# Projections, overflow check and attention of a transformer block joined in one program block, and two more row groups normalised inside the attention

## What is computed

```
x = x + 0.5 * FFN(layernorm(x))      # "first FFN"
x = x + Attention(layernorm(x))
x = x + 0.5 * FFN(layernorm(x))      # "second FFN"
```

## Time and profile before

| | us |
|---|---|
| median of 3 runs | 1558.76 |
| the profiled execution's own time | 1560.47 |
| its span, first to last instruction | 1558.4 |
| first FFN, about | 0 to 490 |
| projections and overflow check | 490 to 583 |
| attention | 583 to 1095 |
| second FFN | 1095 to 1558 |

### The profile page before, as it was taken

How to read it: one execution, slowest core, us unless ns; L and a number is a source line. 1 busy time by engine, 2 the same in 40 slices (tenths; PEclk the granted TensorE clock), 3 DMA queues, 4 the chain that set the end, 5 groups by cost and what they waited for, 6 DMA issues and landing times. The chain is left out here.

```text
span 1558.4 us, 26615 instructions
## 1 busy us (share of the span) xinstructions
PE 1492.9 (96%) x9977; PEld 1043.3 (67%) x9977; DVE 895.8 (57%) x1963; ACT 976.9 (63%) x1332; POOL 549.6 (35%) x477
## 2 busy tenths in 40 slices
PE   4999999999997979999999999999899999999997
PEld 3788888888986863333343343343688889888896
DVE  6788776666755971231145152033788867666663
ACT  7322254455434869999999999998622245445542
POOL 2000255666544971211111111120300045666645
PEclk9999999999998998999999999999899999999999
DMA  8222266676646689415246063121511246666653
GB/s 279 76 67 68 84 175 153 148 153 158 147 80 157 230 273 182 85 19 84 35 90 136 30 125 59 25 69 41 167 50 62 69 153 150 151 151 150 162 113 41
DMA packets 121377, 181.05 MB, mean 116 GB/s; under 512 B 19040, under 2 KB 83040, under 8 KB 118496
## 3 DMA queue, kind: packets, MB, share of 16 engines
q1 hardware_dynamic: 92784, 130.56, 32.0%
q0 software_dynamic: 28464, 48.78, 15.3%
HBM read 123.73 MB, written 55.57 MB: 115 GB/s over the span
## 5 line engine op out<-in xcount | busy, mean ns | idle before, releaser
L2140 ACT ACTIVATE 8258_pr<-8258_pS 128x1024 f32<-128x1024 f32 x448 | 420.6, 1195 | 7.4 <-PE 8258_pS L2059 7.4
L2090 PE MATMUL 8258_pO<-8258_pr,6357_vres 128*32 128x512 f32 x1792 | 238.2, 605 | 0.0
L2059 PEld LDWEIGHTS 8258_pS<-sq_rows,sk_rows 50*128 50x128 f32 x896 | 77.9, 185 | 184.4 <-ACT 8258_pr L2140 133.4
L2059 PE MATMUL 8258_pS<-sq_rows,sk_rows 50*128 50x512 f32 x896 | 184.7, 470 | 6.6 <-PEq L1716 5.6
L346 PE MATMUL 115_pGU<-columns_XT,weights_wts 128*128 128x512 f32 x384 | 152.7, 398 | 1.0 <-DVE columns_XT L1118 0.8
L346 PE MATMUL 15280_pGU<-columns_XT,weights_wts 128*128 128x512 f32 x384 | 152.7, 398 | 1.0 <-DVE columns_XT L1118 0.8
L2153 POOL TENSOR_SCALAR_AFFINE_SELECT 8258_pr<-8258_pr 128x512 f32<-128x512 f32 x32 | 20.5, 641 | 371.1 <-ACT 8258_pr L2140 371.1
L347 PE MATMUL 15280_pGU<-columns_XT,weights_wts 128*128 128x512 f32 x384 | 149.7, 390 | 0.0
L347 PE MATMUL 115_pGU<-columns_XT,weights_wts 128*128 128x512 f32 x384 | 149.7, 390 | 0.0
L348 PE MATMUL 115_pGU<-columns_XT,weights_wts 128*128 128x512 f32 x384 | 149.6, 390 | 0.0
L348 PE MATMUL 15280_pGU<-columns_XT,weights_wts 128*128 128x512 f32 x384 | 149.6, 390 | 0.0
(11 more groups left out here) (393 smaller groups left out, 3491.3 us busy)
## 6 DMA issues: line engine op xcount, KB each, us to landing
115_raw_g<-WgT SPq DMA_DIRECT2D x16, 512.0 KB
115_raw_u<-WuT SPq DMA_DIRECT2D x16, 512.0 KB
115_raw_d<-WdT SPq DMA_DIRECT2D x16, 512.0 KB
q_rows<-rows_halves SPq DMA_DIRECT2D x8, 1024.0 KB, 4.9
k_rows<-rows_halves SPq DMA_DIRECT2D x8, 1024.0 KB, 5.1
15280_raw_g<-WgT SPq DMA_DIRECT2D x16, 512.0 KB
15280_raw_u<-WuT SPq DMA_DIRECT2D x16, 512.0 KB
15280_raw_d<-WdT SPq DMA_DIRECT2D x16, 512.0 KB
```

The costliest lines, as they stand in the source:

```text
L2059: m = t_.matmul(to[:, e, :], key, query, start=True, stop=True)
L2090: m = t_.matmul(pO[e * 32:(e + 1) * 32, j % 2, off:off + wd], vres[:, (g // GB) * TPB + kt, at:at + 32], from_(e), start=n == first[j], st ...
L2140: s_exp.done(a.activation(to, pS[:, u % RING, :, :], ACT.Exp, scale=HD ** -0.5))
```

## The change

- The three functions return their engine functions instead of opening a block, and `attn` puts them behind each other in one block. Where the barriers stood, an engine waits for the semaphores that it needs: all four checking engines for the flag, TensorE for the last rotations, squares and v copies, ScalarE for the last rotations and, at unit 7 (pair 4), for all lower parts, VectorE for the last v product ahead of its memset. Buffers move so that the first units write over nothing that is still read.
- The end of the projections is put in another order: unit 12's lower part goes from GpSimd to VectorE (`POOL_LOW` 12), the last two squares and rotations are interleaved, the norms stand between the halves of the last v product, and VectorE finds the flag before the lower parts of units 13 to 15. ScalarE loads the Exp table before its last v copy. TensorE issues 24 matmuls of ones (`FILL`).
- SyncE issues the second halves of heads 0 to 3 behind the stores of units 12, 13 (two) and 14.
- `READY` is 7: quads 5 and 6 are normalised in the attention, quad 6 into a buffer of its own (`apart`), without a wait for its store, and with two table stores. The second FFN normalises quad 7 alone, GpSimd splits one shared weight before its one table store and two behind it.

```diff
-AHEAD, READY = 4, 5
+AHEAD, READY, APART = 4, 7, 6
...
-            ring = lambda q: (q - (ready > 0)) % KN
+            ring = lambda q: (q - ready + AHEAD if ready else q) % KN
...
+
+            def row(q, j, cols):
+                if q == APART and q < ready:
+                    return self.apart[:, j // 2, :].rearrange("p (t d) -> p t d", d=D)[:, j % 2, cols]
+                return xn(q)[:, j, cols]
...
-                    deviation(ready)
-                    columns(0)
-                    deviation(ready + 1)
-                    normalize(ready)
-                    columns(1)
-                    normalize(ready + 1)
-                    deviation(ready + 2)
-                    columns(2)
-                    normalize(ready + 2)
-                    for q in range(3, J):
+                    for q in range(ready, J):
+                        deviation(q)
+                        if q > ready:
+                            normalize(q - 1)
+                        columns(q - ready)
...
-                    statistics(ready)
-                    statistics(ready + 1)
-                    scale(ready)
-                    low_columns(0)
-                    scale(ready + 1)
-                    statistics(ready + 2)
-                    low_columns(1)
-                    scale(ready + 2)
-                    for q in range(2, J):
+                    for q in range(ready, J):
+                        statistics(q)
+                        scale(q)
+                        low_columns(q - ready)
+                    for q in range(J - ready, J):
                         low_columns(q)
...
-                        s_wh.done(g.tensor_copy(weight(1, w, 0), raw[w][:, :, :]))
-                    s_wh.wait(g, w + 1)
+                        s_whs.done(g.tensor_copy(weight(1, w, 0), raw[w][:, :, :]))
+                        s_whs.wait(g, w + 1)
+                    else:
...
+                if ready:
+                    split_shared(0)
                 for q in range(ready, J):
-                    if ready:
-                        split_shared(q - ready)
                     g.wait_ge(*s_xn.at(q - ready + 1))
...
                 if ready:
-                    g.wait_ge(*self.s_table.at(READY))
+                    split_shared(1)
+                    split_shared(2)
+                    g.wait_ge(*self.s_table.at(READY + 1))
...
-            POOL_LOW = 2 * J - 3
+            POOL_LOW = 2 * J - 4
+            FILL = 24
+            REST_AFTER = ((6, 0), (6, 1), (6, 1), (7, 0))
...
+                        for hh, at in enumerate(REST_AFTER):
+                            if at == (q, half_):
+                                self.load_head(sp, 0, hh, slice(S // 2, S), self.s_rest)
...
                     s_sq.wait(t_, n - 2)
+                    s_turn.wait(t_, n - 2)
...
-                    values(q)
+                    if q + 1 < J:
+                        values(q)
+                values(J - 1, (0,))
                 norms(J - 1)
+                values(J - 1, (1,))
                 t_.wait_ge(*s_top.at(1))
                 s_tt.done(t_.transpose(pN[0:1, 0:P], top[:, :], self.ident[:, :]))
...
+                for _ in range(FILL):
+                    t_.matmul(pX[:, 0, 0:P], self.ones[:, :], self.ones[:, :], start=True, stop=True)
...
                 def square(n):
-                    a.wait_ge(*s_turn.at(n + 1))
...
-                    square(4 * q + 2)
-                    high(2 * q)
-                    square(4 * q + 3)
-                    value(q)
+                    if q + 1 < J:
+                        square(4 * q + 2)
+                        high(2 * q)
+                        square(4 * q + 3)
+                        value(q)
+                square(4 * J - 1)
+                square(4 * J - 2)
+                high(2 * J - 2)
+                value(J - 1, (0,))
+                a.activation(warm[:, :], self.eps[0:1, :], ACT.Exp)
+                value(J - 1, (1,))
                 high(2 * J - 1)
-                a.activation(warm[:, :], self.eps[0:1, :], ACT.Exp)
...
-                    v.wait_ge(*s_Q.at(n + 1))
+                    v.wait_ge(*(s_sq.at(n) if n == 4 * J - 1 else s_Q.at(n + 1)))
...
-                    s_lo.wait(v, n // 2 - 2)
+                    s_lo.wait(v, min(n // 2 - 2, POOL_LOW))
...
-                    rotate(4 * q + 2)
-                    rotate(4 * q + 3)
+                    if q + 1 < J:
+                        rotate(4 * q + 2)
+                        rotate(4 * q + 3)
...
                 k = (2 * J - 1) % 3
+                low(POOL_LOW)
+                v.wait_ge(*s_last.at(1))
+                rotate(4 * J - 2)
+                rotate(4 * J - 1)
                 s_turn.wait(v, 4 * J)
-                v.tensor_tensor(turns[k][:, 0, :], turns[k][:, 0, :], turns[k][:, 2, :], ALU.subtract)
-                s_last_y.done(v.tensor_tensor(turns[k][:, 1, :], turns[k][:, 1, :], turns[k][:, 3, :], ALU.add))
-                low(POOL_LOW)
                 largest(J - 1)
                 s_norm.wait(v, J // 2)
                 s_top.done(v.tensor_reduce(top[:, :], norm[:, :], AX.X, ALU.max))
-                low(POOL_LOW + 1)
+                v.tensor_tensor(turns[k][:, 0, :], turns[k][:, 0, :], turns[k][:, 2, :], ALU.subtract)
+                s_last_y.done(v.tensor_tensor(turns[k][:, 1, :], turns[k][:, 1, :], turns[k][:, 3, :], ALU.add))
                 v.wait_ge(*s_tt.at(1))
                 s_flag.done(v.tensor_reduce(best[:, :], pN[0:1, 0:P].rearrange("p (a h) -> p a h", a=2), AX.X, ALU.max))
                 v.wait_ge(*s_flag.at(1))
                 s_flag.done(v.tensor_tensor(prod[:, :], best[:, 0:1], best[:, 1:2], ALU.mult))
                 v.wait_ge(*s_flag.at(2))
                 s_flag.done(v.tensor_scalar(self.unsafe[:, :], prod[:, :], SAFE_NORMS, None, ALU.is_gt))
-                low(POOL_LOW + 2)
-                v.wait_ge(*s_flag.at(3))
-
...
+                for n in range(POOL_LOW + 1, 2 * J):
+                    low(n)
...
             def guarded(eng, body):
+                eng.wait_ge(*self.s_flag.at(3))
                 r = eng.value_load(self.unsafe[0:1, 0:1], min_val=0, max_val=1)
...
 
-            @blk.sync
-            def _(sp):
+            def on_sync(sp):
...
+                    sp.wait_ge(*self.s_kept.at(2 * NQ))
+                    sp.wait_ge(*self.s_last.at(2 * NQ - self.POOL_LOW))
...
+            self.apart = yb[:, :, APART % QB, :, :].rearrange("p c k d -> p c (k d)")
...
+                if m == APART:
+                    norm_at[quiet(max(root_at) + 4, 1)] = m
+                    table_at[max(norm_at) + 1] = m
+                    continue
...
-                for hh in range(GH):
-                    self.load_head(sp, 0, hh, slice(S // 2, S), self.s_rest)
...
                     sp.wait_ge(*self.s_norm.at(m + 1))
-                    self.s_table.done(sp.dma_start(table[m], mine_of(m)))
+                    if m == APART:
+                        for c in range(DC):
+                            self.s_table.done(sp.dma_start(table[m][:, 2 * c:2 * c + 2, :], self.apart[:, c, :].rearrange("p (t d) -> p t d", d=D)))
+                    else:
...
+                t_.wait_ge(*self.s_turned.at(4 * NQ))
+                t_.wait_ge(*self.s_squared.at(4 * NQ))
+                t_.wait_ge(*self.s_kept.at(2 * NQ))
...
+                a.wait_ge(*self.s_turned.at(4 * NQ))
                 for u, (kind, a_, b_) in enumerate(units):
                     a.wait_ge(*s_S.at(u + 1))
+                    if (kind, a_) == ("pair", 4):
+                        a.wait_ge(*self.s_low.at(self.POOL_LOW))
+                        a.wait_ge(*self.s_last.at(2 * NQ - self.POOL_LOW))
...
-                        to = prs[:, a_ % 2, 2 * b_:2 * b_ + 2, :]
+                        to = prs[:, (a_ + 1) % 2, 2 * b_:2 * b_ + 2, :]
...
                 def normalize(m):
-                    s_out[m % 4].wait(v, m // 4 + 1)
+                    if m != APART:
+                        s_out[m % 4].wait(v, m // 4 + 1)
                     for j in range(4):
-                        i = v.tensor_scalar(mine_of(m)[:, j, :], mine_of(m)[:, j, :], root[:, j:j + 1], shift[:, j:j + 1], ALU.mult, ALU.add)
+                        i = v.tensor_scalar(rows_of(m, j), mine_of(m)[:, j, :], root[:, j:j + 1], shift[:, j:j + 1], ALU.mult, ALU.add)
                     self.s_norm.done(i)
 
+                v.wait_ge(*self.s_values.at(2 * NQ))
...
-            self.projections(st, x)
-            self.exact_shift()
-            self.attention(x, out)
+            project, shift, attend = self.projections(st, x), self.exact_shift(), self.attention(x, out)
+            with self.nc.Block() as blk:
+                @blk.sync
+                def _(sp):
+                    project["sync"](sp)
+                    shift["sync"](sp)
...
+                @blk.tensor
+                def _(t_):
+                    project["tensor"](t_)
```

(2 more changed lines are left out.)

108 lines of the change are left out of this document (65 added, 43 removed).

## The result

The changed kernel takes 1547.31 us (median of 4 runs, 1546.60 to 1547.98), the kernel before 1558.26 us on the same chip (4 runs, 1557.34 to 1560.07): a ratio of 0.9928, 95% interval 0.9911 to 0.9945. (The 1558.76 given further above is the median of three of these four.) It is 10.95 us faster; 9.2 were forecast, and 1549.6 with a range of 1546.6 to 1554.2. The profiled execution took 1546.60, its span is 1544.9.

What follows compares the result with a forecast made beforehand. TensorE was busy for 96% of the span, leaving its gaps and slow stretches at two hand-overs. Savings of 3.0 + 2.1 + 1.5 + 2.6 = 9.2 us took 1558.76 to 1549.6, range 1546.6 to 1554.2.

Steps and rivals of the forecast that it cites:

- Step 1: End of the projections: fewer lower parts and a new order on VectorE bring the flag 3.1 us earlier, called 3.0.
- Step 2: From the flag to the first scores: without barriers and the work between, 2.1 us saved, bounds 1.0 to 2.3.
- The load and branch stay: Between flag and first scores: register load and branch remain, 2.15 us with a semaphore's 0.1.
- Step 3: Start of the attention: TensorE's clock stays at its upper level and ScalarE's two waits go, 1.5 us, bounds 0 to 1.8.
- the first rival: The clock falls all the same, in the pause or the thin first units: 1551.1 us, chance 0.13.
- the prediction's own signs of being wrong: TensorE wait at unit 18, quad 6 reaching into the last turn, clock 0.50 behind 578, or barrier-like wait for v copies.
- Step 4: Start of the attention: second-half loads issued among the last stores, and other moved waits, cost 0, cover 7 us.
- "slower" rival: Second halves of heads 0 to 3 reach unit 18 late: each us beyond 593 costs one, 1561 with 17 us; chance 0.04.
- The cover of `heads_of(0)`: VectorE at the attention's start waits for all stores to about 591, next needed at about 599: cover 7 us.
- Step 5: End of the attention: VectorE's work on quads 5 and 6 fits ahead of the last turn, cost 0, cover 2.1 us.
- Step 6: Start of the second FFN: work on two quads gone, 2.6 us saved, bounds 1.5 to 3.5.
- twice that, about 4, at the lower: Second FFN's turns: TensorE's pace of 1.80 us taken as about 4 at the lower clock, lasting until 1104.4.

## Why the prediction was right, step by step

**Step 1, the flag: 3.0 forecast, 3.11 measured.** Rotation 30 began 3.89 us behind rotation 28 instead of 4.88 (0.99 earlier; forecast 0.95), and the flag came 5.54 behind rotation 30 (forecast 5.55). VectorE was first at the SBUF, as taken: its lower part took 1.22, and GpSimd's operation, begun 0.16 later, took 2.21 instead of 1.30. By the Trainium skill, page "SBUF — State Buffer", section "Who interferes with whom", the two exclude each other for a whole instruction; the trace agrees, with 0.91 us of holding, where VectorE's operation still had 1.06 to run. ScalarE waited 0.28 us for GpSimd behind it (571.19), off the way to the flag. The run with the flag behind the lower parts shows that all of it is on the path.

**Step 2, flag to scores: 2.1 forecast, 2.85 measured**, outside the bounds of 1.0 to 2.3. The mechanism was right: with the barriers back the piece is 7.0. The mis-sized term is "The load and branch stay", 2.0 by the earlier trace rows: with the semaphore the whole way is 1.41 instead of 2.15, since the load itself took 0.48 instead of 1.17. Why it was fast is open. With the slow load, in the run with the flag behind the lower parts, the way is 2.06, and step 2 would give 2.2, almost as forecast. The v copies I put at 576.1 to 577, which is 9.8 to 10.7 behind the start of rotation 28; they ended at 9.94, 0.5 behind the flag and well within the way of load and branch.

**Step 3, the clock: 1.5 forecast, 1.19 in the profiled run, and less on the whole.** The statement that failed is "so I expect it to stay at its upper level". It fell at 580.3, not in the pause but in the thin first units, as the first rival said, and a clock of 0.50 behind 578 was one of the prediction's own signs of being wrong; only it came back after 3.4 us rather than 13.7. How soon it comes back is not the same from run to run. Of six traces with the same code up to here, first scores to 10th exp took 9.64, 9.69, 10.27, 10.73, 10.94 and 11.68 us, mean 10.5, with the clock low for 3.4 to 13.6 us. Against the one trace of before (10.88) this step is worth 0.4 on the mean, and in one of the six it is a loss. Neither the ones nor the pause could be shown to set it.

**Step 4, loads moved: cost 0 forecast, 0 measured.** No wait of TensorE on a DMA stands in 590 to 603 us. What the prediction missed is what the step is for. It called the loads' place free; left in the old place they cost a wait of 3.13 and a second fall of the clock, about 5 us by that trace. The "slower" rival had the right transfer, the right unit and about the right moment (593); the change stays clear of it, since its last load is issued by 584.62: with 4.9 on the way, my estimate from that trace, it is there at 589.5, 3 us ahead of unit 18's scores (592.57). The cover of `heads_of(0)` was thinner than said, 2.65 us instead of 7: the last store went out at 584.66, as forecast, and VectorE waited for it until 592.95.

**Step 5, quads 5 and 6 in the attention: cost 0 with a cover of 2.1 forecast; measured 0, with 2.17 idle** ahead of the last turn. The attention is as long as before to 0.2 us.

**Step 6, the start of the second FFN: 2.6 forecast, 4.03 measured**, above the upper bound of 3.5. Turn 2 came 1.13 earlier from the first (forecast 1.25), the end from turn 7 to the first shared product took 4.09, as forecast. The mis-sized term lies between: turn 2 to turn 7 was forecast at 11.7 by "twice that, about 4, at the lower" clock, which was to last 9.5 us from the first turn, and took 10.16. The clock was back after 5.8. Turn 4, put at 2.8 behind turn 3 with half of it at the lower level, came 1.84 behind it, at the upper; that is 1.0 of the 1.5. The other 0.6 is turn 3, 2.92 behind turn 2 instead of 3.5. Turns 2 and 3 were not at TensorE's pace: with the clock held up they come at the same moments to 0.01 us, because VectorE's subtractions and ScalarE's copies set them. Why the clock came back earlier is not shown. Undoing the two quads, with their order, costs 3.5 by the run with the old order, in which the clock was back after 9.0.

Sum: 3.1 + 2.85 + 1.2 + 4.0 = 11.2 in the profiled run, 10.4 with step 3 at 0.4, and 10.95 on the medians, against 9.2. Both misses that count, steps 2 and 6, were on the cautious side, and for the same reason: a duration was carried over from a row of before, the load's 1.17 and the clock's 9.5, that did not hold after the change. That the sum came within 1.8 us is in part luck: the mechanism of step 3 failed and fell short by 0.3 to 1.1, which made up for part of what steps 2 and 6 gave above their forecast, and 0.7 of that was the fast load, which nothing in the prediction gave a reason for.

## What to carry to other kernels

A hand-over between stages is a chain, and its parts are worth their price only together: here the early flag behind barriers gave 0.4 us, early loads behind barriers came out 3 us slower than before, and one block without the early loads lost some 5 us again, because whatever is not brought along becomes the next wait. Only the one block with the late flag kept something alone: rotation 28 to the first scores 14.89 us, against 16.80 before. Before calling a moved transfer free, ask when its reader will come in the kernel *after* the change. And ahead of costing a stretch at an engine's slow clock, check that this engine is what the stretch waits for, and whether its clock is still slow there after the change; a run in which the clock is held up tells the first.

## What the hardware showed beside that

- The load of one SBUF word into a register took either 0.48 to 0.55 or 1.10 to 1.25 us. In the changed kernel it took 484, 505, 545 and 481 ns on the four queues, at 574.4 to 585.2. With the barriers back all four began within 0.1 us and took 1166 to 1251. But a single queue took 1145 (VectorE's, with the copies first) and 1161 (SyncE's, with the loads back) as well. The traffic of the DMA engines alone does not decide: SyncE's load of 481 ns began while they moved 406 GB/s (585.2 to 585.7), TensorE's of 1137 ns, with the flag behind the lower parts, at 270 (577.6 to 578.1). What does decide I can't say.
- The granted clock came back after 3.4 us in one run and after 13.6 in another of the same code. A median over runs averages that; one profile does not, and two of my readings of single profiles (the ones, and the size of step 3) did not survive the next trace.
- In three of the fourteen traces, some 150 us into the attention, TensorE stood still for 0.9 to 1.2 us between two products with the values, with nothing released to it, and ScalarE waited 1.4 to 1.6 us. It is in kernels whose code there is the same as in those without it. TensorE's timeline with the quads back:
```profile
721.34 1.04 PE L2123 MATMUL 6372_pO<-6372_pr,6357_vres 128*32 128x512 f32 x2
723.58 1.06 PE L2123 MATMUL 6372_pO<-6372_pr,6357_vres 128*32 128x512 f32 x6 [1.19 <-issue]
```
Its cause is left open.
- A table load of 1.28 us was free where ScalarE had nothing to do yet (1086.50 in the changed kernel, the root could not begin before 1088.51), and stood on ScalarE's path with its whole length one instruction later (1092.04, columns first).
